# Query and key rows 17 KB apart in scratch memory, stored in eight pieces per tensor

## What is computed

```python
mod = (silu(c) @ wmod).reshape(16, 6, 1, -1)          # sa, ca, ga, sb, cb, gb
h = layernorm(x) * (1 + ca) + sa
q, k, v = heads(h @ Wq + bq), heads(h @ Wk + bk), heads(h @ Wv + bv)
scores = (q k^T + q . pos_emb[l - r] + k . pos_emb[l - r]) / sqrt(D)
x = x + ga * layernorm_gb(softmax(scores) v @ Wo + bo + h)
h = layernorm(x) * (1 + cb) + sb
x = x + gb * sum over the top 2 of 8 experts of (h @ w_e + b_e)
```

## Time and profile before

| | before |
|---|---|
| median of 3 runs | 2890.61 us (2886.45 to 2895.83) |
| profiled execution | 2886.97 us, span 2885.2 us |
| PE busy | 2521.4 us, 87% |
| DVE busy | 2055.5 us, 71% |
| POOL busy | 1883.5 us, 65% |
| ACT busy | 1627.6 us, 56% |
| mean granted TensorE clock | 0.900 |
| DMA | 773.59 MB, mean 268 GB/s |

### The profile page before, as it was taken

The page is one execution under the profiler, slowest core; times in us unless marked ns, Lnnn a source line. Parts: engine busy times, 40 slices in busy tenths (PEclk is TensorE's granted clock), DMA queues, the critical chain, the costliest instruction groups (busy, mean ns, idle before and its releaser), DMA issues. The chain is left out here.

```text
span 2885.2 us, 53492 instructions
## 1 busy us (share of the span) xinstructions
PE 2521.4 (87%) x19084; PEld 1753.8 (61%) x19084; DVE 2055.5 (71%) x5771; ACT 1627.6 (56%) x2069; POOL 1883.5 (65%) x1535
## 2 busy tenths in 40 slices
PE   3988688788878888599999999999999499999998
PEld 1655477677767777366666666666666355555553
DVE  4767277667767777577777777777777388888885
ACT  1645556566556666277878778788877222222222
POOL 2333356565765564488888888888888356666664
PEclk7999777778778778599999999999999799999999
DMA  3688799999999999999999999999998312222210
GB/s 117 226 296 269 259 401 386 378 400 385 398 393 387 376 404 388 316 328 317 302 313 308 312 310 306 304 306 301 314 301 266 132 68 77 77 77 77 77 48 24
DMA packets 301960, 773.59 MB, mean 268 GB/s; under 512 B 37608, under 2 KB 104496, under 8 KB 258048
## 3 DMA queue, kind: packets, MB, share of 16 engines
q1 hardware_dynamic: 277152, 660.82, 66.6%
q10 hardware_dynamic: 17888, 86.27, 9.2%
q0 software_dynamic: 6656, 23.07, 2.3%
HBM read 417.39 MB, written 352.63 MB: 267 GB/s over the span
## 5 line engine op out<-in xcount | busy, mean ns | idle before, releaser
L952 POOL TENSOR_SCALAR t_neg<-t_neg,t_low 128x512 f32<-128x512 f32 x512 | 793.6, 1563 | 121.5 <-DVE t_low L1153 117.2
L1153 DVE CUSTOM_DVE_ANT_1 t_neg<-t_ps,t_r 128x512 f32<-128x512 f32 x1024 | 667.6, 686 | 250.5 <-issue 245.5
L1215 ACT ACTIVATE t_eT<-t_pt 128x1024 f32<-128x1024 f32 x512 | 524.3, 1024 | 211.6 <-PE t_pt L1072 211.0
L1072 PE MATMUL t_pt<-t_ident,t_neg 128*128 128x128 f32 x4096 | 617.3, 273 | 4.7 <-POOL t_neg L952 4.2
L1072 PEld LDWEIGHTS t_pt<-t_ident,t_neg 128*128 128x128 f32 x4096 | 516.4, 142 | 82.9 <-POOL t_neg L952 5.9
L1537 PE MATMUL e_pX<-e_we,e_h2T 128*128 128x512 f32 x1024 | 455.8, 596 | 14.3 <-DVE e_even L1745 14.3
L1060 PE MATMUL t_ps<-t_kb,t_qa 96*128 96x512 bf16 x1024 | 399.1, 390 | 62.0 <-DVE t_low L1153 37.2
L831 DVE TENSOR_TENSOR d_r<-d_pq,d_r 128x1024 f32<-128x1024 f32 x256 | 299.6, 1219 | 139.0 <-ACT d_r L804 103.8
L1205 ACT ACTIVATE t_neg<-t_neg,t_low 128x512 f32<-128x512 f32 x512 | 369.2, 721 | 46.3 <-DVE t_low L1153 46.3
L831 DVE TENSOR_TENSOR ad_nat<-d_pq,ad_nat 128x1024 f32<-128x1024 f32 x256 | 298.6, 1218 | 121.0 <-ACT ad_nat L804 99.5
L706 POOL COPY ad_nat<-ad_nat 32x2048 f32<-32x2048 f32 (+1 forms) x156 | 294.3, 1886 | 104.6 <-DMA ad_nat<-q_by_place_scratch 98.3
(11 more groups left out here) (156 smaller groups left out, 3269.6 us busy)
## 6 DMA issues: line engine op xcount, KB each, us to landing
t_r<-r_scratch SPq DMA_DIRECT2D x1024, 256.0 KB, 6.5
r_scratch<-d_r SPq DMA_DIRECT2D x128, 1024.0 KB, 9.3
r_scratch<-ad_nat SPq DMA_DIRECT2D x128, 1024.0 KB, 7.0
ad_nat<-q_by_place_scratch ACTq DMA_DIRECT2D x78, 256.0 KB, 6.3
q_rows_scratch<-a_part SPq DMA_DIRECT2D x16, 768.0 KB, 4.7
k_rows_scratch<-a_part SPq DMA_DIRECT2D x16, 768.0 KB, 6.7
q_by_place_scratch<-ad_nat SPq DMA_DIRECT2D x6, 2048.0 KB, 16.8
k_by_place_scratch<-ad_nat SPq DMA_DIRECT2D x6, 2048.0 KB, 19.4
```

Of the source, the lines that this page charges most:

```text
L952: nc.gpsimd.tensor_scalar(neg[:, j % RING, t, :], neg[:, j % RING, t, :], low[:, j % RING, t:t + 1], None, ALU.subtract).then_inc(pool_sub, 1)
L1072: last = nc.tensor.transpose(p_t[t // 2][:, t % 2, c, :], neg[:, j % RING, t, c * P:(c + 1) * P], ident[:])
L1153: nc.vector.tensor_tensor_reduce(out=neg[:, j % RING, t, :].rearrange("p (c r) -> p c r", r=TB), in0=p_s[t % 2][:].rearrange("p (c r) -> p ...
L1215: nc.scalar.activation(to, p_t[half][:], ACT.Exp, scale=(1.0 if half else -1.0)).then_inc(exped, 1)
```

## The change

The scratch tensors of the query and key rows become [batch, 48, 16 x 512 + 512]: the rows begin 17 KB apart and the last KB of each is not used. A head's rows of one depth index no longer follow on those of the next at the same distance, so the 128 partitions can't be addressed as one dimension; the store becomes eight DMAs, one for each of the eight depth indices of a half, each of 16 partitions by 6 by 1 KB (96 KB). The waits for these stores count 8 x 16 in place of 16. The loads in attention read the same rows from their new places with the same number of DMAs.

```diff
@@ projections, store_rows
-                    to = rows_d[i][b].rearrange("(c r) h w -> c (r h) w", c=3 * KC).rearrange("c p w -> p c w")
-                    sp.dma_start(to, part[:, u, i].rearrange("p s c w -> p (s c) w")).then_inc(rows_stored[u][i], 16)
+                    to = rows_d[i][b, :, 0:H * S].rearrange("(c r) (h w) -> r h c w", c=3 * KC, w=S)
+                    for r in range(P // H):
+                        sp.dma_start(to[r], part[r * H:(r + 1) * H, u, i].rearrange("p s c w -> p (s c) w")
+                                     ).then_inc(rows_stored[u][i], 16)
@@ projections, end of SP's work
-                        sp.wait_ge(rows_stored[u][i], 16 * (nb // 2))
+                        sp.wait_ge(rows_stored[u][i], 16 * P // H * (nb // 2))
@@ projections, first_part
-                    later(act, rows_stored[u][i], 16 * (b // 2))
+                    later(act, rows_stored[u][i], 16 * P // H * (b // 2))
@@ attention, load
-                        src[b, stored:stored + rows, first:first + H // 2].rearrange("r h w -> r (h w)")
+                        src[b, stored:stored + rows, first * S:(first + H // 2) * S]
@@ program
-    rows_d = [scratch(f"{x}_rows_scratch", [NB, SD, H, S], BF16) for x in "qk"]
+    rows_d = [scratch(f"{x}_rows_scratch", [NB, SD, H * S + S], BF16) for x in "qk"]
```

## The result

| | before | after |
|---|---|---|
| median | 2889.48 us (12 runs, 2886.02 to 2895.83) | 2895.26 us (12 runs, 2888.62 to 2903.98) |
| ratio | | 1.0022, 95% interval 1.0014 to 1.0029 |
| profiled execution, its span | 2886.97, 2885.2 us | 2888.62, 2886.7 us |
| first v store to first DMA of the distances | 258.51 us | 261.90 us |
| that DMA to the first load of attention | 862.72 us | 862.10 us |

The change costs 0.22%, some 6 us. The prediction said 2888.6 us, a gain of 2 us. The measured time lies inside its range (2879 to 2899), but the sign is wrong, and the cost is clear of the interval of the measurement. The profiled execution happens to be the shortest of the twelve, 6.6 us under the median, so its span shows too little of the cost; how much of this is the place where the cost arises and how much is scatter of other stages was the first question for the experiments.

What follows compares the result with a forecast made beforehand. The prediction had TensorE nearly always busy in projections and attention, and DMA share 0.99 in the distances. Projections +2.0 (+0.7 + 1.3) and attention -4.0 sum to -2.0: 2890.6 - 2.0 = 2888.6 us, range 2879 to 2899.

Steps and rivals of the forecast that it cites:

- Steady part of the projections: Ordinary batches of the projections: eight pieces take SP 3.5 us, covered by its idle time, so 0.
- SP is the bound: Projections: at 0.97 us a piece SP needs 16.8 us in a 15.2 us batch, +24, 2915 us; rival, chance 0.07.
- The group boundary: Projections, batches 7 and 8, where SP is not free: +0.7 us for q, 0 for the k and h stores.
- the q store: Group boundary: its pieces delay the 2 MB stores' issue by 3.1 us, mostly covered by earlier data: +0.7, bounds 0 and +3.1.
- the drain to 174.4: Group boundary: 1.28 MB of v and q data at 390 GB/s take 3.3 us from 171.05, ending at 174.4.
- the k store: Group boundary, store at 192.00: 3.5 us of issue in place of 1.29, hidden by the ring's backlog: 0, uncovered +2.2.
- the h stores behind: Group boundary: batch 9's h store comes up to 5 us later, held by 5.2 us of slack: 0.
- The end of the projections: Last k store: its last piece is issued at 322.0 and lands at 323.7, against 322.4: +1.3, upper bound +3.1.
- Attention's start: First query and key loads in attention: 17 KB pitch cures half the slow reads, -4.0, bounds 0 and -8.1.
- the pitch does nothing: Attention's start: the 17 KB pitch gains nothing, leaving +2.0, 2892.6 us; rival, chance 0.22.
- Distances and shifted scratches: Scratches behind start elsewhere; rival: 1% of the distances, 8.6 us to either side, 2880 or 2899 us, chance 0.06.
- boundary and end at their upper bounds and nothing gained: Projections: group boundary and end cost their upper bounds, +8.4, with no gain in attention: 2899.0 us; rival, chance 0.05.

Runs made afterwards that it cites:

- pieces_elsewhere: Kernel before, 16 KB pitch, with stores in eight pieces except batches 7, 8, 9 and the last key store: 258.26 us to the distances, ratio 1.0002.
- pieces_q7: Kernel before, 16 KB pitch, with only batch 7's query store in eight pieces: 260.30 us to the distances, ratio 1.0007.
- pieces_k7: Kernel before, 16 KB pitch, with only batch 7's key store in eight pieces: 259.96 us to the distances, ratio 1.0012.
- pieces_8_9: Kernel before, 16 KB pitch, with only the stores of batches 8 and 9 in eight pieces: 258.58 us to the distances, ratio 1.0008.
- pieces_boundary: Kernel before, 16 KB pitch, with only the stores of batches 7, 8 and 9 in eight pieces: 262.33 us to the distances, ratio 1.0019.
- h_first: Kernel before, with the h stores of batches 8 and 9 issued ahead of the 2 MB stores: 258.30 us to the distances, ratio 1.0001.

## Why the prediction was wrong, point by point
**Steady part of the projections: right.** 0 was forecast with SP's idle time as cover; the period stayed 15.22 us and pieces_elsewhere lost nothing. The price of a piece was low: 0.44 us from the table store, 0.55 measured. The prediction calls that store the nearest row without saying that it carries 32 KB, a third of a piece. It also leaves out that the packets slow down (the share goes from 0.68 to 0.76 at 228 and 226 GB/s), which costs nothing here since the engines have room. The rival "SP is the bound" needed 0.87 and didn't come, though in the batches right behind the boundary, where SP had fallen behind, it issues without a pause.

**The group boundary: mis-sized, this is the error.** For the q store I had +0.7 us, by the argument that the 2 MB stores stand behind the data of v and q anyway. It is +2.0 (pieces_q7). Two terms failed: 8 x 0.55 in place of 3.5 us; and the drain to 174.4, which let the rows flow at 390 GB/s while the pieces, by the reading above, only come at SP's pace. For the k store I had 0, "hidden by the ring's backlog", with +2.2 as price without cover. It is +1.7 (pieces_k7): the cover is real but it is 4.2 us long and the issue takes 7.8, not 3.5; I had taken the piece's price from an idle queue, although show that one store costs SP 1.29 us there, and a piece of an eighth of its size costs as much. For the h stores behind I had 0 within 5.2 us of slack, and pieces_8_9 shows +0.3, within the scatter: right. Together +0.7 against +4.0; in the four traces with all the pieces it is +1.5 to +5.7 over the 140.5 us of the kernel without pieces, from the v store of batch 7 to that of batch 15. Of the Trainium skill's rule against small, split transfers ("DMA: Bandwidth & Descriptors", Rules for kernel authors) the direction was right. The fixed 2.0 us that the section Anatomy of one DMA gives, for DMAs issued by GpSimd and not by SP, did not come in series: the last k pieces land in 2.3 to 2.6 us each and are issued 0.5 us apart.

**The end of the projections: right in kind.** +1.3 was forecast, +2.1 came. Issue 3.8 and not 3.1 + 0.4 us, and 2.4 us to landing and not 1.7: 3.4 more issue less 1.3 for the shorter landing (3.7 to 2.4) is 2.1.

**Attention's start: wrong, and it turned the sign.** I took -4.0, half of a cure, without a row that halved it. It is 0: the throughput went from 186 to 200 GB/s, within the scatter of 165 (pieces_boundary) to 202 (h_first) over kernels with the 16 KB pitch, the loads alone at 17 KB change nothing (ratio 1.0000), and so the rival "the pitch does nothing" (given 0.22) was the right one here. The halved throughput of this stretch is real and stays unexplained; my argument from it, that rows falling on the same part of the memory cause it, had against it that single loads of the same pitch land in 6.1 us, and that should have weighed more. The gain that the Trainium skill ("DMA: Bandwidth & Descriptors", Latency and other measured facts) gives for padding large power-of-two pitches, measured there from 512 KiB up and with 4 KiB, did not come at 16 KB with 1 KB of padding.

**Distances and shifted scratches: right.** 0; the shift alone gives 1.0006 (0.9997 to 1.0015). But the distances scatter from 859 to 869 us over the traces of all kernels, whatever is changed; this is what makes one profiled execution a poor witness of 6 us in the total, and why the stretch of the projections was the better measure.

With the measured terms the sum is 4.0 + 2.1 + 0 = +6.1, against 5.8 (the medians: 2895.26 - 2889.48). By the size of the change the case "boundary and end at their upper bounds and nothing gained" (+8.4, chance 0.05) was nearest, before "the pitch does nothing" (+2.0); what came is between the two, nothing gained and the middle of the costs. What is open: why the batches behind the boundary caught up 2.7 to 3.8 us more in the changed kernel's first trace than in the other two with all pieces; how the cost at the boundary divides between slow issuing and slow packets; and why the engines move only 165 to 202 GB/s at attention's start.

## What to carry to other kernels
As far as these runs go, a DMA that is split without need costs issue time wherever the queue of its engine or the DMA engines have no slack, and nothing elsewhere: here 25 of the 32 split stores are free, the four of batches 8 and 9 can't be told from free, and the two ahead of the big stores and the last one of the stage pay for all. Price the issue by a row taken under the load in which it will run, and the cover by its length: a backlog of 4 us doesn't hide 8 us of issuing. Don't take a mean of issue times for a pace before looking whether it mixes a full and an empty queue. And look at throughput and busy share together: the one divided by the other shows slow packets where each alone shows nothing. And before a layout is paid for, let a kernel read by it alone: that takes one run, and it showed the gain to be nothing.

## What the runs showed of the hardware
A single issue on SP's queue took 0.33 to 0.37 us in most places and 0.97 us in some right behind another. In a row of eight or six it took 0.47 to 0.64 us on average. While the DMA engines had older work queued (at 387 GB/s) it took 1.2 to 1.9 us for 96 KB, and 1.29 for 768 KB, so this hardly depended on what it carried; the first issue behind three stores of 2 MB took 5.4 to 6.4 us, for 512 KB (h) and, in h_first, for 768 KB (k). A piece of 96 KB landed in 2.3 to 2.6 us at the end of the projections, the 768 KB store in 3.7. Pieces that take every eighth partition are issued more slowly than those of neighbouring ones (5.13 against 4.53 us for eight), but their packets are faster (263 against 217 GB/s for a full share of the engines; 336 where each DMA takes all 128 partitions). Rows of 8 KB read at a pitch of 17 KB in place of 16 make no difference beyond the interval of 0.1%.
